# One block in each of eight groups gathered by the sync engine, row by row, in a graph attention and expert kernel

## The chip, the cores and the metric
The kernel runs on one core of a Trainium2 chip. The metric is its time on the device in microseconds, as the median of several runs; beside it stands the profile of one execution, whose span is measured from its first to its last instruction. The engines are named as in the profile: PE (matmuls), PEld (weight loads of PE), DVE, ACT, POOL (GpSimd) and SP (the sync engine). SPq rows are instructions that SP's queue issues.

## What is computed
A graph attention layer over 3125 nodes and 50000 edges, sorted by target `dst`, and behind it a layer of eight experts. Every edge needs the row of its source node: 256 features and 8 attention scores.

```python
h = (x @ W).reshape(N, H, C)                       # x: layer-normed nodes, N=3125, H=8, C=256
e = leaky_relu(a_src[src] + a_dst[dst], 0.2)
e = exp(e - segment_max(e, dst)[dst])
alpha = e / (segment_sum(e, dst)[dst] + 1e-16)
out = segment_sum(h[src] * alpha[:, :, None], dst).mean(axis=1) + bias
x = x + out
x = x + moe(layernorm(x))                          # top 2 of 8 experts, gelu between two 256x256 layers
```

## The kernel before, in words
The normed node features and the source scores are stored in a table in HBM, `node_table`, 264 floats a row (`TILES*P` rows). The edges are cut in 392 blocks of `BLK` = 128, and the blocks in nine groups by `GROUP_PLAN`: seven of 48 blocks, one of 32, one of 24. The ring in SBUF, `rows`, has `ROOM` = 96 slots of a block, one edge to a partition.

POOL gathers a block with one indirect DMA (`gather`, L730 to L736): 128 rows at the indices `idx[:, b]`. It goes through the groups in order. From group 2 it waits at every fourth block until PE is done with the blocks that stood in these slots (`block_done`). In group 0 it gathers 32 blocks, then sends 25 scatters of scores (L788) and a gather of start rows, then the other 16 blocks.

DVE does for each group g, in program order: `flags(g)` (from the scan line `dst_scan[g % 2]`, target numbers of the group; the first instruction, L1619, counts `scan_read`), `scores(g)` (L1641, waits until all blocks of the group have landed, semaphore `got`), the softmax steps, and `spreads(g)`, which makes PE's weights four blocks at a time. At g = 6 there is an exception: `flags(6)`, `flags(7)` and `flags(8)` stand one after the other, all ahead of `scores(6)`. PE multiplies a block in four matmuls (L973) and starts a group when its first weights are there. ACT drains sums and stores them in `agg_table`. When all groups are through, PE projects the sums (L1097) and the experts follow.

SP issues its transfers in program order. In the stretch with the groups these are: `node_scores_stored` (L568) and the score table (L571), the zeroed starts read back (L575, waits for the 25 scatters), a bias and four small weights (L577 to L581), and then `load_scan(g)` for g = 2 to 8 (L551, L554, L557), each of which waits until `flags(g - 2)` has read the buffer:

```python
n, ch = kb_of(g) * BLK, chunks_of(g)
if g >= 2:
    sp.wait_ge(scan_read, g - 1)
...
for g in range(2, GROUPS):
    load_scan(g)
```

The order on DVE at the end of the groups:

```python
for g in range(GROUPS):
    if g < GROUPS - 2:
        flags(g)
    if g == GROUPS - 3:
        flags(GROUPS - 2)
        flags(GROUPS - 1)
    ...
    scores(g)
```

Of the kernel before, what the change touches and what calls it, by code (L numbers as in the profile page):

```python
# [11 lines left out]
PE, POOL = mybir.EngineType.PE, mybir.EngineType.Pool  # L12
# [33 lines left out]
UNROLL = 5  # L46

# [17 lines left out]
def gat_moe_kernel(nc, x, src, dst, W, att_src, att_dst, gnn_bias, router_w, w1, b1, w2, b2, out):  # L65
# [68 lines left out]
    with ExitStack() as ctx:  # L134
# [125 lines left out]

        start_rows = sb("start_rows", [TURN_ROWS, H])
# [167 lines left out]
        got = [sem(f"got{j}") for j in range(4)]  # L429
        e_ready, eT_done, pieces_ready, pieces_done, fac_ready, fac_done = (  # L430
# [79 lines left out]
        def got_by(g):  # L510
            return 16 * sum(blocks_of(i) for i in range(g + 1) if got_of(i) == got_of(g))
# [4 lines left out]
        def _(sp):  # L516
# [46 lines left out]
            for i in range(TILES // UNROLL):  # L563
                sp.wait_ge(xn_ready, (i + 1) * UNROLL)
                sp.dma_start(node_table[:, 0:D].rearrange("(t p) d -> p t d", p=P)[:, i * UNROLL:(i + 1) * UNROLL, :],
                             xn[:, i * UNROLL:(i + 1) * UNROLL, :]).then_inc(xn_stored, 16)
            sp.wait_ge(score_ready, 1)
            sp.dma_start(node_table[:, D:].rearrange("(t p) h -> p t h", p=P), score_all[:, :, 0:H])\  # L568
                .then_inc(node_scores_stored, 16)
            sp.wait_ge(score_ready, 2)  # L570
            sp.dma_start(score_table.rearrange("(t p) h -> p t h", p=P), score_all[:, :, H:2 * H])\  # L571
                .then_inc(target_scores_stored, 16)

# [4 lines left out]
            for k in range(2):  # L578
                sp.dma_start(router_sb[:, k, :], router_w[:, k * P:(k + 1) * P].rearrange("e p -> p e"),
                             allow_slow_non_contiguous=True).then_inc(in_small, 16)  # L580
                sp.dma_start(b1_sb[:, :, k], b1[:, k * P:(k + 1) * P].rearrange("e p -> p e"),  # L581
                             allow_slow_non_contiguous=True).then_inc(in_small, 16)
            for g in range(2, GROUPS):
                load_scan(g)

# [82 lines left out]
        def _(pool):  # L668
# [61 lines left out]
            def gather(g, first, last):  # L730
                for s in range(first, last):
                    if g >= 2 and s % QUAD == 0:
                        pool.wait_ge(block_done, first_of[g] - ROOM + s + QUAD + 1)
                    b = first_of[g] + s
                    pool.indirect_dma_start(rows[:, slot_of(b), :], None, node_table,  # L735
                                            bass.IndirectOffsetOnAxis(idx[:, b:b + 1], 0)).then_inc(got[got_of(g)], 16)  # L736
# [608 lines left out]
        def _(dve):  # L1345
# [288 lines left out]
            def scores(g):  # L1634
# [3 lines left out]
                dve.wait_ge(got[got_of(g)], got_by(g))  # L1638

# [503 lines left out]
```

## Time and profile before
| | us |
|---|---|
| median of three runs | 1154.89 |
| lowest and highest | 1150.71, 1158.80 |
| span of the profiled execution | 1025.7 |
| busy: PE, DVE, ACT, POOL | 669.8, 680.2, 355.3, 673.2 |
| gathers of node rows (L735), 392 | 408.7 busy |
| largest items of the chain that ended last, by line | POOL L735 22%, PE L1097 12%, PE L973 5% |

The table's last rows are from the page of the profile. "Busy" doesn't count waits, nor the issuing of DMAs by SP and ACT. The groups are gathered from 57.7 us to 620.8 us of the span.

### The profile page before, as it was taken

How to read it: one execution, taken by the hardware profiler on the slowest of the kernel's cores; microseconds unless marked ns; L12 is line 12 of the kernel's file. 1: busy time of each engine (PE TensorE's matmuls, PEld its weight loads, DVE VectorE, ACT ScalarE, POOL GpSimd, SP SyncE). 2: the span in 40 equal slices, each digit the busy share in tenths (PEclk: the TensorE clock that was granted, in tenths of full speed). 3: DMA queues.
4: the chain of work that ended last, by engine and by line, in shares of the span. 5: the costliest groups of instructions: out<-in, count | busy, mean ns of one | idle time of the engine just before them, and what ended most of it. 6: DMA issues, size and time to landing. Idle time of an engine off the chain costs nothing.

```text
span 1025.7 us, 15575 instructions
## 1 busy us (share of the span) xinstructions
PE 669.8 (65%) x3740; PEld 602.6 (59%) x3741; DVE 680.2 (66%) x1860; ACT 355.3 (35%) x831; POOL 673.2 (66%) x705
## 2 busy tenths in 40 slices
PE   4982012427646275471754687599999998678996
PEld 3981001327546175461654677588888887567995
DVE  6888318727757276572875778657678968775663
ACT  3720003337645364231331110023323222335664
POOL 5787777777777777777777771235073375557786
PEclk9999999978878687676876898899999999889998
DMA  9634153567867677555664456198986862366873
GB/s 347 217 80 96 24 117 103 163 223 255 260 204 241 206 249 220 168 180 156 187 182 134 142 165 254 40 337 310 346 321 225 298 230 83 80 133 99 134 130 58
DMA packets 96985, 189.62 MB, mean 185 GB/s; under 512 B 24743, under 2 KB 54802, under 8 KB 95804
## 3 DMA queue, kind: packets, MB, share of 16 engines
q0 software_dynamic: 31680, 70.52, 28.3%
q1 hardware_dynamic: 50256, 72.93, 21.0%
q10 hardware_dynamic: 14960, 45.16, 11.4%
q8 instruction: 35, 0.57, 0.2%
q14 instruction: 54, 0.44, 0.1%
HBM read 124.74 MB, written 64.74 MB: 185 GB/s over the span
## 4 chain that ended last, share of the span: by engine, by line
PE 29%; POOL 26%; DVE 19%; issue 13%; DMA 8%; ACT 1%; POOLq 1%; DVEq 1%; ACTq 0%; SPq 0%; PEldq 0%; PEld 0%
POOL ring L735 22%; PE banks L1097 12%; PE banks L973 5%; PE banks L1172 3%; PE banks L1156 3%; DMA ring<-node_table,idx 3%; POOL starts_table L788 2%; DMA out<-ring 2%; PE banks L927 2%; DVE arena L1373 2%; DMA ring<-agg_table 1%; PE banks L914 1%; DMA arena<-in_src 1%; POOL slot_table L835 1%; PE banks L1144 1%
## 5 line engine op out<-in xcount | busy, mean ns | idle before, releaser
L735 POOL DMA_INDIRECT ring<-node_table,idx x392 | 408.7, 1043 | 121.4 <-issue 115.0
L973 PE MATMUL banks<-arena,ring 128*128 128x160 f32 x1568 | 256.9, 328 | 39.3 <-ACT banks L1264 18.7
L973 PEld LDWEIGHTS banks<-arena,ring 128*128 128x128 f32 x1568 | 245.2, 212 | 51.8 <-issue 51.4
L1258 ACT COPY arena<-banks 128x400 f32<-128x400 f32 x200 | 88.4, 493 | 322.6 <-PE banks L973 204.9
L1097 PE MATMUL banks<-ring 128*128 128x256 f32 x544 | 120.5, 381 | 0.0
L849 POOL DMA_INDIRECT out<-ring x56 | 89.8, 1603 | 33.9 <-DMA out<-ring 18.0
L1097 PEld LDWEIGHTS banks<-ring 128*128 128x128 f32 x544 | 102.7, 190 | 13.2
L1758 DVE TENSOR_TENSOR arena<-hot,arena 128x640 f32<-128x640 f32 x84 | 64.6, 823 | 34.8 <-PE banks L973 34.5
L980 PE MATMUL banks<-ident,edge_e 128*128 128x128 f32 x25 | 7.2, 417 | 119.7 <-DVEq L1649 119.6
L980 PEld LDWEIGHTS banks<-ident,edge_e 128*128 128x128 f32 x25 | 3.9, 201 | 121.9 <-DVEq L1649 121.9
L1156 PEld LDWEIGHTS banks<-ring 128*128 128x128 f32 x448 | 60.6, 200 | 20.0 <-DVE ring L2022 16.8
L1156 PE MATMUL banks<-ring 128*128 128x128 f32 x448 | 63.3, 287 | 13.2 <-DVE ring L2022 13.0
L835 POOL DMA_INDIRECT slot_table<-arena,slots x50 | 57.2, 1143 | 14.5 <-issue 13.7
L1172 PE MATMUL banks<-arena,ring 128*128 x224 | 62.4, 403 | 1.5 <-issue 1.4
L1641 DVE TENSOR_TENSOR edge_z<-ring,arena 128x384 f32<-128x384 f32 (+2 forms) x9 | 4.3, 478 | 82.4 <-DMA ring<-node_table,idx 82.4
L1097 PE MATMUL banks<-ring,arena 128*128 128x256 f32 x256 | 57.0, 381 | 0.0
L830 POOL COPY arena<-tags 128x3 f32<-128x3 f32 x25 | 3.6, 194 | 80.6 <-DVEq L1910 80.6
L1262 ACT COPY banks<-zeros 128x400 f32<-128x400 f32 x100 | 50.4, 504 | 11.6 <-ACT arena L1258 10.2
L1097 PEld LDWEIGHTS banks<-ring,arena 128*128 128x128 f32 x256 | 48.4, 190 | 6.3
L2046 DVE SCALAR_TENSOR_TENSOR ring<-banks,job_w,ring 128x256 f32<-128x256 f32 x56 | 27.1, 484 | 35.8 <-PE banks L1172 29.7
L1264 ACT COPY banks<-zeros 128x400 f32<-128x400 f32 x100 | 49.7, 497 | 0.0
L1172 PEld LDWEIGHTS banks<-arena,ring 128*128 128x128 f32 x224 | 40.2, 200 | 7.1 <-issue 3.4
(411 smaller groups left out, 1183.1 us busy)
## 6 DMA issues: line engine op xcount, KB each, us to landing
agg_table<-arena ACTq DMA_DIRECT2D x100, 400.0 KB
ring<-agg_table SPq DMA_DIRECT2D x25, 1600.0 KB, 8.5
ring<-slot_table SPq DMA_DIRECT2D x56, 130.0 KB, 2.6
ring<-node_table,idx POOLq DMA_INDIRECT x392
ring<-in_x SPq DMA_DIRECT2D x8, 640.0 KB, 13.2
arena<-in_L_ffn_w SPq DMA_DIRECT2D x16, 256.0 KB, 8.7
node_table<-ring SPq DMA_DIRECT2D x5, 640.0 KB, 5.4
ring<-in_L_gnn_W ACTq DMA_DIRECT2D x1, 2048.0 KB, 9.0
```

What stands on the lines that cost most here:

```text
L735: pool.indirect_dma_start(rows[:, slot_of(b), :], None, node_table, bass.IndirectOffsetOnAxis(idx[:, b:b + 1], 0)).then_inc(got[got_of(g)] ...
L835: pool.indirect_dma_start(slot_table, bass.IndirectOffsetOnAxis(slots[:, k, t:t + 1], 0), tn[t % TN_RING], None).then_inc(sent[t % TN_RING ...
L849: pool.indirect_dma_start(out, bass.IndirectOffsetOnAxis(xs[j % XS_RING][:, D:D + 1].bitcast(I32), 0), ybuf[j % Y_RING], None, bounds_chec ...
L973: m = pe.matmul(columns[:, k, bass.ds(at * (UNIT * H), SPREAD * H)], lhs[:, k * P:(k + 1) * P], weights, start=False, stop=True, skip_grou ...
L1097: m = pe.matmul(bank[proj_bank(t)][:, 0:D], aggt[t % AGG_RING][:, k * H + h, :], W_sb[:, k, h * C:(h + 1) * C], start=(k == 0 and h == 0), ...
L1156: m = pe.matmul(h_bank[j % 2][:, f * P:(f + 1) * P], w1_now[j % 2][:, k, f * P:(f + 1) * P], xsT[j % 2][:, k, :], start=(k == 0), stop=(k ...
L1172: m = pe.matmul(y_bank[j % 2][:, 0:D], h_sb[j % 2][:, f, :], w2_sb[:, bass.ds(e, 1), f, :].rearrange("p e n -> p (e n)"), start=(f == 0), ...
L1258: act.copy(stage[j][:, k * SLOTS * H:(k + 1) * SLOTS * H], views[k]).then_inc(drained, 1)
L1262: act.copy(views[0], zeros[:, 0:1].to_broadcast([P, SLOTS * H]))
L1264: act.copy(views[1], zeros[:, 0:1].to_broadcast([P, SLOTS * H])).then_inc(acc_free, 1)
L1758: dve.tensor_tensor(spread[:, s:s + QUAD, :].rearrange("p s (d h) -> p s d h", h=H), hot[:, q * QUAD:(q + 1) * QUAD, :].unsqueeze(3).to_br ...
L2046: dve.scalar_tensor_tensor(ybuf[j % Y_RING], y_bank[j % 2][:, 0:D], job_w[j % 3][:, 1:2], b2_now[j % 3], ALU.mult, ALU.add).then_inc(y_rea ...
```

## The change
SP gathers block 3 (`SP_AT`, the last of the first four) of groups 0 to 7. For each it loads the 128 source numbers of the block into `sp_src` (two buffers, `load_sources`), reads eight of them at a time into registers, and issues one DMA of one row (264 floats) for each edge, to the slot and partition where POOL's gather would have put it. POOL leaves these eight blocks out; DVE waits for both before `scores(g)`.

```diff
+ROWS_OF_SP = range(0, 8)
+SP_AT = QUAD - 1
+SP_WORDS = 8
+SP_FIRST = 48
...
         def got_by(g):
-            return 16 * sum(blocks_of(i) for i in range(g + 1) if got_of(i) == got_of(g))
+            return 16 * sum(blocks_of(i) - (i in ROWS_OF_SP) for i in range(g + 1) if got_of(i) == got_of(g))
...
+            def gather_rows(g, first, last):
+                b = first_of[g] + SP_AT
+                if first == 0:
+                    sp.wait_ge(in_sp_src, 16 * (g + 1))
+                    if g + 1 in ROWS_OF_SP:
+                        load_sources(g + 1)
+                    if g >= 2:
+                        sp.wait_ge(block_done, b - ROOM + 2)
+                for j0 in range(first, last, SP_WORDS):
+                    cols = slice(g % 2 * BLK + j0, g % 2 * BLK + j0 + SP_WORDS)
+                    _, nodes = nc.values_load_multi_w_load_instructions(sp_src[0:1, cols], engines=[SP], min_val=0, max_val=N - 1,
+                                                                       skip_runtime_bounds_check_because="every entry of src is a node")
+                    for n, node in enumerate(nodes):
+                        j = BLK - 1 - (j0 + n)
+                        sp.dma_start(rows[j:j + 1, slot_of(b), :], node_table[bass.ds(node, 1), :]).then_inc(got_sp[g % 2], 16)
+
+            def load_sources(g):
+                at = EP - (first_of[g] + SP_AT + 1) * BLK
+                sp.dma_start(sp_src[0:1, g % 2 * BLK:(g % 2 + 1) * BLK], src[at:at + BLK].rearrange("(i n) -> i n", i=1))\
+                    .then_inc(in_sp_src, 16)
+
+            load_sources(0)
             sp.wait_ge(score_ready, 1)
             sp.dma_start(node_table[:, D:].rearrange("(t p) h -> p t h", p=P), score_all[:, :, 0:H])\
                 .then_inc(node_scores_stored, 16)
+            sp.wait_ge(node_scores_stored, 16)
+            sp.wait_ge(xn_stored, 16 * (TILES // UNROLL))
+            sp.wait_ge(va_summed, 2)
+            gather_rows(0, 0, SP_FIRST)
             sp.wait_ge(score_ready, 2)
             sp.dma_start(score_table.rearrange("(t p) h -> p t h", p=P), score_all[:, :, H:2 * H])\
                 .then_inc(target_scores_stored, 16)
+            gather_rows(0, SP_FIRST, BLK)
...
+            sp.wait_ge(steps_ready, 1)
+            gather_rows(1, 0, BLK)
             for g in range(2, GROUPS):
                 load_scan(g)
+                if g in ROWS_OF_SP:
+                    gather_rows(g, 0, BLK)
...
                     b = first_of[g] + s
+                    if g in ROWS_OF_SP and s == SP_AT:
+                        continue
...
                 dve.wait_ge(got[got_of(g)], got_by(g))
+                if g in ROWS_OF_SP:
+                    dve.wait_ge(got_sp[g % 2], 16 * BLK * (g // 2 + 1))
```

SP's queue before, from the four small loads to the end of the groups; the scan lines of groups 2 to 8 stand together (`x5` and the three rows behind it):

```order
L579 DMA router_sb<-in_L_ffn_router_w 128x8x1
L581 DMA b_sb<-in_L_ffn_b 128x8x1
L551 DMA dst_scan<-dst_table 128x1x386 [waits scan_read] x5
L551 DMA dst_scan<-dst_table 128x1x258 [waits scan_read]
L554 DMA dst_scan<-dst_table 88x1x258 [waits scan_read]
L557 DMA dst_scan<-dst_table 8x257
L608 DMA ring<-in_L_gnn_W 128x2x2048 [waits block_done]
```

SP's queue now, at the start of group 1's rows (line numbers are those of the changed file; ISA is the register instruction that forms an address):

```order
L614 DMA router_sb<-in_L_ffn_router_w 128x8x1
L616 DMA b_sb<-in_L_ffn_b 128x8x1
L593 DMA sp_src<-in_src 1x128 [waits in_sp_src,steps_ready]
L585 TENSOR_LOAD sp_src
L589 ISA
L589 DMA ring<-node_table 1x264
L589 ISA
L589 DMA ring<-node_table 1x264
```

A block is 16 such TENSOR_LOADs, each followed by eight pairs of ISA and DMA. At the end of group 7's rows there stands now:

```order
L589 ISA
L589 DMA ring<-node_table 1x264
L562 DMA dst_scan<-dst_table 88x1x258 [waits scan_read]
L565 DMA dst_scan<-dst_table 8x257
L647 DMA ring<-in_L_gnn_W 128x2x2048 [waits block_done]
```

The scan line of group 8 (L554 and L557 before, L562 and L565 now) stands behind the 128 rows of group 7, whose first waits for PE's first four blocks of group 5; each of the scan lines of groups 3 to 7 stands behind the rows of the group ahead of it.

## Rows read from the trace of the kernel before
**Rows 1.** The page: the span, and the chain that ended last, by line.
```profile
span 1025.7 us, 15575 instructions
...
POOL ring L735 22%; PE banks L1097 12%; PE banks L973 5%; PE banks L1172 3%; PE banks L1156 3%; DMA ring<-node_table,idx 3%; POOL starts_table L788 2%; DMA out<-ring 2%; PE banks L927 2%; DVE arena L1373 2%; DMA ring<-agg_table 1%; PE banks L914 1%; DMA arena<-in_src 1%; POOL slot_table L835 1%; PE banks L1144 1%
```
**Rows 2.** Grouped by line, 164 to 547 us: count, busy us, mean ns, idle before.
```profile
L735 POOL DMA_INDIRECT ring<-node_table,idx x288 | 293.8, 1020 | 89.7 <-issue 85.2 <-PE banks L973 4.6
```
**Rows 3.** Waits, DVE's and SP's queue: us in total, times, longest.
```profile
DVE edge_z L1641 <- DMA ring<-node_table,idx: 82.4, 9, 16.5
...
SPq L551 <- DVE arena L1619: 310.4, 6, 66.1
```
**Rows 4.** Timeline of DVE: start us, duration us, what, idle before.
```profile
528.23 0.56 DVE L1619 TENSOR_TENSOR arena<-dst_scan 128x385 f32<-128x385 int32 x1
...
536.39 0.43 DVE L1619 TENSOR_TENSOR zero_rows<-dst_scan 128x257 f32<-128x257 int32 x1
...
548.76 0.56 DVE L1641 TENSOR_TENSOR edge_z<-ring,arena 128x384 f32<-128x384 f32 x1 [8.98 <-DMA ring<-node_table,idx]
...
592.85 0.43 DVE L1641 TENSOR_TENSOR edge_z<-ring,arena 128x256 f32<-128x256 f32 x1 [0.18 <-DMA ring<-node_table,idx]
...
626.39 0.36 DVE L1641 TENSOR_TENSOR edge_z<-ring,arena 128x192 f32<-128x192 f32 x1 [2.04 <-DMA ring<-node_table,idx]
```
**Rows 5.** Timeline of SP's queue: score table, starts, last small load, last scan line.
```profile
86.39 0.36 SPq L571 DMA_DIRECT2D score_table<-score_all  x1
...
139.11 0.34 SPq L575 DMA_DIRECT2D arena<-starts_table  x1
...
150.19 1.18 SPq L581 DMA_DIRECT2D b_sb<-in_L_ffn_b  x1
...
528.81 0.85 SPq L554 DMA_DIRECT2D dst_scan<-dst_table  x1
529.70 0.47 SPq L557 DMA_DIRECT2D dst_scan<-dst_table  x1
```
**Rows 6.** Timeline (first row), then single lines: count, ns min/median/max, first and last start.
```profile
2.08 0.55 SPq L524 DMA_DIRECT2D arena<-in_dst  x2
...
L524 SPq DMA_DIRECT2D arena<-in_dst x2: 228/255/282, 2.1 to 2.4; - x2
...
L654 SPq FUSED_REGOPS  x8: 37/37/42, 899.7 to 907.8; - x8
L654 SPq MOVE slot_table<-zero_rows x8: 29/29/29, 899.8 to 907.8; - x8
L654 SPq DMA_DIRECT2D slot_table<-zero_rows x8: 332/332/370, 899.8 to 907.9; - x8
...
L653 SPq TENSOR_LOAD <-fill_row x8: 263/270/507, 899.1 to 906.9; - x8
...
L841 POOLq TENSOR_LOAD <-job_wait x55: 315/326/604, 884.4 to 1016.1; - x55
...
L740 POOLq TENSOR_LOAD <-far x9: 289/296/889, 211.8 to 652.1; - x9
```
**Rows 7.** Timeline of PE: group 5 begins; the projection begins.
```profile
516.46 5.83 PE L973 MATMUL banks<-arena,ring 128*128 128x160 f32 x26 [2.52 <-DVE arena L1758]
...
668.37 3.83 PE L1097 MATMUL banks<-ring 128*128 128x256 f32 x17
```
**Rows 8.** DMA issues: KB each, median us from issue to landing.
```profile
dst_scan<-dst_table SPq DMA_DIRECT2D x1, 129.0 KB, 3.9
```
**Rows 9.** The page, DMA queues: packets, MB, share of 16 engines.
```profile
q0 software_dynamic: 31680, 70.52, 28.3%
q1 hardware_dynamic: 50256, 72.93, 21.0%
q10 hardware_dynamic: 14960, 45.16, 11.4%
```

More of the change, by code:

```diff
@@ L11 @@
 AX_X = mybir.AxisListType.X
-PE, POOL = mybir.EngineType.PE, mybir.EngineType.Pool
+PE, POOL, SP = mybir.EngineType.PE, mybir.EngineType.Pool, mybir.EngineType.SP
 P = 128
@@ L259, in gat_moe_kernel @@
         zero_rows = sb("zero_rows", [P, SLOT])
+        sp_src = sb("sp_src", [1, 2 * BLK], I32)
         start_rows = sb("start_rows", [TURN_ROWS, H])
@@ L429, in gat_moe_kernel @@
         got = [sem(f"got{j}") for j in range(4)]
+        in_sp_src = sem("in_sp_src")
+        got_sp = [sem(f"got_sp{j}") for j in range(2)]
         e_ready, eT_done, pieces_ready, pieces_done, fac_ready, fac_done = (
```

## The prediction
> **What bounds the kernel now.** I read the page first: its span, and the chain that ended last by line [rows 1]. POOL's gather at L735 is the largest item of the chain, 22%, three times any DMA item and ahead of every matmul line. Then the grouped instructions between 164 and 547 us, which is where groups 1 to 6 are gathered [rows 2]: 288 gathers, 293.8 us busy and 89.7 us idle, of which 85.2 is "issue", time in which POOL waited for nothing. So POOL gathers without a break: (293.8 + 89.7) / 288 = 1.33 us for one block of 128 edges, 64 us for a group. No other engine is near full in that stretch. The waits say the same from the other side [rows 3]: DVE waits nine times, once for each group, 82.4 us in all, for gathered rows to land. In the stages before and after (scores, projection, experts) the change alters nothing but what arrives late.
>
> Two more things must be read, because the change puts much work on the SP queue. First, what SP does in that stretch: it waits, 310 us in six waits at L551, for DVE to have read the last `dst_scan` buffer at L1619 [rows 3]. It looks like an idle queue. Second, what hangs on SP's few transfers there. DVE's timeline [rows 4] shows it for group 6: at 528.23 DVE reads the scan line of group 6 (flags), at 536.39 already that of group 8, and only behind that comes `scores(6)` at 548.76, after 8.98 us of waiting for the gather, so flags(8) ended at 539.78. The program has flags(6), flags(7), flags(8) ahead of scores(6) on DVE. The scan line of group 8 was sent by SP at 528.81 and 529.70 [rows 5], as soon as flags(6) had freed the buffer. So the cover of that transfer is 9 us and no more.
>
> **The change, part by part.**
> *Removed:* eight gathers on POOL, at 1.33 us each: 10.6 us. This is the whole possible gain; since POOL has no break, each of them would come off the end if all else kept up. Block 3 of groups 0 to 5 is 8.0 us of it, of groups 0 to 6 9.3 us.
>
> *Added on SP:* eight blocks of 128 single-row DMAs. None is in the trace of before, so I build the pitch of one row from its nearest rows [rows 6]. A register-addressed DMA of SP (L654) takes FUSED_REGOPS 0.037, MOVE 0.029 and the DMA itself. The DMA is 0.332 there for 128 partitions; the four single-row DMAs of L524 take 0.228 to 0.282, median 0.255. Two of them in a row take 0.55, so the gap between instructions is 0.55 - 0.51 = 0.04, three per row. Pitch: 0.037 + 0.029 + 0.255 + 3 x 0.04 = 0.44 us. I take the single-row duration because shape is what differs here, and registers seem to cost nothing extra in the DMA. The bounds are 0.41 (the 0.228) and 0.52 (the 0.332). For each 8 rows there is a TENSOR_LOAD: 0.27 for one word; POOL's loads of four words take 0.326 against 0.296 for one, 0.01 a word, so 0.32 for eight, 0.36 with a gap. A block is R = 128 x 0.44 + 16 x 0.36 = 56.4 + 5.8 = 62.2 us. (Bounds: 58 and 73.) That is just under POOL's 64 us a group: SP goes from idle to saturated.
>
> *Where the rows run:* group 0's are cheap. The first 48 go from 57 to about 80, ahead of the score store whose data came at 86; the other 80 need 39 us more, to 126; SP would wait until 139.11 for L575 anyway [rows 5]. All that moves is 1.3 us earlier. The four small loads behind L575 keep SP until 151.37; less 1.3 is 150.1, where rows(1) begin. From here SP is one chain: each later group adds a scan line (0.5, as the one at 529.70 [rows 5]), one load of addresses (0.255) and gaps, 0.85 in all. Rows of group 7 end at 150.1 + 0.3 + 6 x 0.85 + 7 x 62.2 = 590.9. The other condition, that rows(7) wait for the first four blocks of group 5 on PE (516.46 [rows 7], less 8.0, plus 16 matmuls at 5.83 / 26 us, 3.6, makes 512.1), would give 512.1 + 62.2 = 574.3, so the queue binds. Ends of rows(2) to rows(6), 276, 339, 402, 465 and 528, lie ahead of POOL's own gathers (before 290 to 547, less up to 9.3), so `scores` of groups 1 to 6 don't wait for rows.
>
> *Moved:* the scan line of group 8. It is now issued behind rows(7), at 590.9 in place of 528.81. Who is queued behind it: SP sends its two DMAs (1.36 us), they land 3.9 us after issue [rows 8], DVE's flags(8) take 539.78 - 536.39 = 3.4, and then only may scores(6) start: 590.9 + 8.7 = 599.6, against 539.5 if nothing were late. DVE, and behind it PE's group 6, stand still for that time, with POOL's gathers of groups 7 and 8 (its first 16) done meanwhile.
>
> *After that:* scores(6) to scores(7) is 592.85 - 548.76 = 44.1, set by DVE itself (0.18 of waiting). Scores(7) to scores(8) is 33.5, of which 2.04 was waiting for the gather [rows 4]; that is now early (the last eight gathers of group 8 need PE's second quad of group 6, 15 us before they are due), so 31.5. Scores(8) begins at 599.6 + 75.6 = 675.2, against 626.39: 48.8 us later. Behind it there is PE's group 8 and then, from 668.37, the projection [rows 7], both moved by the same amount.
>
> *Sum:* the POOL saving is used up in the wait; the end moves by +48.8. The profiled execution spans 1025.7 us; the runs have a median of 1154.9, so 129.2 us lie around the span, and nothing in the change touches them. 1154.9 + 48.8 = 1203.7, span 1074.5.
>
> What the skill says of such rows: the Trainium skill, DMA: Bandwidth & Descriptors, "Why a DMA increments its semaphore by 16 and not by 1", says that a single-row DMA may run on one DMA engine alone, always the lowest-numbered. By that rule all 1024 rows share one ring; no row here names an engine, and its price is the third rival's below, worked out from rows.
>
> **Range of the main case.** With the 0.228 DMA and 0.31 a load R is 58, the queue ends at 561.5 and PE's condition binds: 512.1 + 58 = 570.1, scores(6) 578.8, +28: 1183. With the 0.332 DMA R is 73, rows(7) end at 666, scores(6) at 675, +124: 1279. Every 0.01 us of pitch is 9 us at the end.
>
> **Rivals.**
> 1. *Each row costs SP a full-size DMA (0.52 us a row).* For it: 128-partition DMAs in this kernel agree at 0.33 to 0.37 and the four short ones are from the first microseconds, before any traffic. Against: the short ones had 2048 and 1344 bytes in one partition, which is the same shape. 1279, or about 1230 to 1290.
> 2. *No change, or faster: SP keeps up.* If rows(7) took less than 30 us, scan line 8 would be issued by 542.1 and the end would not move (542.1 + 8.7 + 75.6 = 626.4, scores(8) as before); below 18.7 us the full 10.6 us come, 1144.3. That needs 0.10 us a row, less than half of the shortest DMA instruction in the trace. This decides the sign: above 0.2 us a row the kernel is slower. A way in which it could still be: SP's instruction durations overlap. L654's eight DMAs start 1.16 us apart with 0.33 of DMA and 0.27 of load in each, more than the durations seen, so they don't.
> 3. *The rows are bound where they are moved, not issued.* Packet times from the page [rows 9]: q1 0.21 x 16 x 1025.7 / 50256 = 0.069 us, q0 0.147, q10 0.125. If all rows were on one ring with two packets each (data, semaphore), and each packet waited for one of q0 and one of q10, a row would take 2 x 0.341 = 0.68, R = 87, rows(7) end at 764, +222: 1377. Unloaded it is 2 x 0.069 = 0.14, far below the pitch of issue. The queues' shares (28.3, 21.0 and 11.4% over the span) say that a packet of each isn't waiting twice per row. The round that this assumes, one packet of each queue in turn, is the rule of the Trainium skill, DMA: Bandwidth & Descriptors, "Queues, rings and completion order"; no row shows it.
> 4. *Only the order bites.* R is smaller than built, some 45 to 57 (addresses found sooner, loads overlapping), and PE's condition sets rows(7): +15 to +27, 1170 to 1182.
>
> **How the numbers follow.** Main case (1183 to 1230) 0.60; rival 1 (1230 to 1290) 0.17; rival 4 0.09; rival 3 0.06; rival 2 0.08, of which within 1% 0.05 and over 1% faster 0.03 (the removed gathers alone are 0.9%, so this needs gathers that also run faster). A measurement of this kernel tells about 1% from no change, 11.5 us. Slower: 0.60 + 0.17 + 0.09 + 0.06 = 0.92. The time predicted is the main case's, 1204. Range 1180 to 1280: the bounds of the pitch; it leaves out rivals 2 and 3 and most of 4, about 0.2. The main case alone: 1183 to 1230.
>
> **What the profile after will show.** SP's single-row DMAs at 0.25 each and 0.44 apart; rows(1) from 150 to 213; rows(7) ending near 591; the scan line of group 8 issued right behind; DVE idle before its third L1619-type read of that group for some 50 us, released by `dst_scan<-dst_table`; nine POOL groups 1.3 us shorter each; PE idle from about 560 to 631 and its clock perhaps lower behind it; POOL gathers of unchanged length. I am wrong if SP's pitch is not 0.41 to 0.52, if DVE does not stand before flags(8), or if `scores` of an early group waits for `got_sp` (then the ring, rival 3, or rival 1 holds).

## The result, and the profile of the changed kernel

| kernel | median, us | range, us | against before |
|---|---|---|---|
| before, beside it | 1153.2 | 1150.7 to 1158.8 | |
| changed | 1424.3 | 1421.0 to 1435.6 | 1.2365, 95% interval 1.2313 to 1.2418 |

The changed kernel is slower by 271 us, where the prediction had 49 (1204, range 1180 to 1280). The sign was right; the size was wrong by a factor of five and the time lies outside the range.

The page of the changed kernel: its span, packets by queue, and the chain that ended last by engine and by line. It answers [rows 1, 9].
```profile
span 1422.4 us, 18781 instructions
...
q1 hardware_dynamic: 52320, 74.02, 15.6%
...
SPq 38%; issue 25%; PE 21%; DVE 9%; another core or an unknown queue 3%; DMA 2%; ACT 1%; DVEq 0%; POOLq 0%; ACTq 0%; PEldq 0%; PEld 0%; POOL 0%
SPq L589 31%; PE banks L1138 10%; SPq L585 6%; PE banks L1014 3%; PE banks L1197 3%; PE banks L1213 3%; PE banks L1185 1%; DVE ring L1436 1%; DMA ring<-agg_table 1%; DVE ring L1488 1%; PE banks L1158 1%; DVE stats L1472 1%; DMA arena<-in_src 1%; DVE arena L1414 1%
```
POOL's gather, 22% of the chain before, is gone from it. SP's queue has its place: L589 (the rows) and L585 (the register loads) are 37%. The waits (us in total, times, longest) say who waits for it, where [rows 3] had gathers:
```profile
DVE edge_z L1684 <- DMA ring<-node_table: 121.8, 5, 32.6
...
DVE zero_rows L1660 <- DMA dst_scan<-dst_table: 64.6, 1, 64.6
...
DVE arena L1660 <- DMA dst_scan<-dst_table: 33.8, 1, 33.8
```
The 64.6 us are the wait that the prediction named, in its place. The first row is the one by which it said that it would be wrong: scores of early groups wait for SP's rows.

What SP's instructions cost, by line: count, ns min/median/max. First in a stretch in which POOL issues 57 DMAs, then in one in which it issues none.
```profile
L589 SPq MOVE ring<-node_table x17: 4/700/1426, 150.4 to 219.7; - x17
L589 SPq DMA_DIRECT2D ring<-node_table x16: 690/700/1396, 152.5 to 216.9; - x16
L589 SPq FUSED_REGOPS  x16: 15/700/709, 154.6 to 218.3; - x16
...
L589 SPq MOVE ring<-node_table x77: 29/29/29, 856.0 to 895.9; - x77
L589 SPq DMA_DIRECT2D ring<-node_table x77: 224/225/261, 856.1 to 896.0; - x77
L589 SPq FUSED_REGOPS  x76: 37/37/37, 856.4 to 895.8; - x76
```
In 856 to 896 the prices are near those of the prediction: 0.225 us for the DMA (forecast 0.255), 0.029 and 0.037 as forecast. In 150 to 220 an instruction takes 0.70 us by the median, with as much between two, a register move of 29 ns too: 16 rows in 70 us. From the first of its row DMAs to the end of the last, a block took 192 us (group 0), 79 (group 1), 94 to 101 (groups 2 to 6) and 66 (group 7, while POOL waited for PE). The slowing is not there from POOL's first DMA at 64.07: from 65 to 70 us POOL issues 4 DMAs and SP starts 30 instructions; from 110 to 115 POOL again issues 4, and SP starts 5.

Nothing in the rows of before looks like that. The runs below show what it goes with: **the time depends on the chip.** The kernel before took 1142 to 1159 us on chips 2 and 13 and 1027 to 1034 us in 16 runs on chip 4. The chip of the first result isn't on record; its times of before are like those of chips 2 and 13. The trace that the prediction was read from, with its span of 1025.7 us [rows 1], looks like one of chip 4. Each comparison below is with runs of before on the same chip, unless it says otherwise.

### The profile page after: what moved, and what is told of

It reads as the page before. It is cut to its first block, busy times and chain, and to the rows that moved or that the text cites. A ratio compares the mean times of both kernels' runs of the same rounds, so it can differ in the third digit from the quotient of the medians.

```text
span 1422.4 us, 18781 instructions
## 1 busy us (share of the span) xinstructions
PE 703.8 (49%) x3740; PEld 633.4 (45%) x3741; DVE 678.6 (48%) x1860; ACT 354.9 (25%) x831; POOL 651.7 (46%) x697
## 4 chain that ended last, share of the span: by engine, by line
SPq 38%; issue 25%; PE 21%; DVE 9%; another core or an unknown queue 3%; DMA 2%; ACT 1%; DVEq 0%; POOLq 0%; ACTq 0%; PEldq 0%; PEld 0%; POOL 0%
SPq L589 31%; PE banks L1138 10%; SPq L585 6%; PE banks L1014 3%; PE banks L1197 3%; PE banks L1213 3%; PE banks L1185 1%; DVE ring L1436 1%; DMA ring<-agg_table 1%; DVE ring L1488 1%; PE banks L1158 1%; DVE stats L1472 1%; DMA arena<-in_src 1%; DVE arena L1414 1%
## 5 line engine op out<-in xcount | busy, mean ns | idle before, releaser
L776 POOL DMA_INDIRECT ring<-node_table,idx x384 | 390.5, 1017 | 500.7 <-PE banks L1014 354.9
L1014 PE MATMUL banks<-arena,ring 128*128 128x160 f32 x1568 | 290.4, 352 | 112.0 <-issue 57.4
L1014 PEld LDWEIGHTS banks<-arena,ring 128*128 128x128 f32 x1568 | 274.9, 232 | 126.8 <-issue 126.5
L1005 PE MATMUL banks<-ident,arena 98*128 98x98 f32 x32 | 7.3, 384 | 117.9 <-DVE arena L1643 117.9
L876 POOL DMA_INDIRECT slot_table<-arena,slots x50 | 54.1, 1081 | 14.5 <-issue 13.7
L1005 PEld LDWEIGHTS banks<-ident,arena 98*128 98x128 f32 x32 | 4.9, 217 | 120.5 <-DVE arena L1643 120.5
L1275 ACT COPY arena<-banks 128x392 f32<-128x392 f32 x8 | 6.9, 858 | 205.6 <-PE banks L1005 205.6
```

Of the source, the lines that this page charges most:

```text
L876: pool.indirect_dma_start(slot_table, bass.IndirectOffsetOnAxis(slots[:, k, t:t + 1], 0), tn[t % TN_RING], None).then_inc(sent[t % TN_RING ...
L1014: m = pe.matmul(columns[:, k, bass.ds(at * (UNIT * H), SPREAD * H)], lhs[:, k * P:(k + 1) * P], weights, start=False, stop=True, skip_grou ...
```

## The experiments

**Theory A:** SP's instruction stream is slowed while POOL issues indirect DMAs, whatever its instructions are. **Theory B:** the transfers of the rows are held back in their queue. With either goes the prediction's order term: group 8's scan line behind the rows of group 7. In what follows rows(g) are SP's 128 row DMAs for group g, and "the starts" are the start rows that SP reads back once POOL's 25 scatters are through.

### Order, addresses, DMAs: four kernels on chip 13

*Scan line of group 8 first.*
```diff
             for g in range(2, GROUPS):
-                load_scan(g)
+                if g < GROUPS - 1:
+                    load_scan(g)
+                if g == GROUPS - 2:
+                    load_scan(GROUPS - 1)
                 if g in ROWS_OF_SP:
                     gather_rows(g, 0, BLK)
```


> The scan line of group 8 is issued ahead of group 7's rows on SP instead of behind them; nothing else changes. Theory A (SP's instruction stream is slowed while GpSimd issues its own indirect loads) and theory B (the transfers of SP's rows are held back in their queue) both leave the rows' pace alone and expect the order's share of the loss back: scores of group 8 then no longer wait for rows(7), which end at 915.4, but for its own flags at 918, so only the aggregation tail moves; 20 to 50 us, thus 1375 to 1405 us. If the order were the whole of the loss (the prediction's own term) it would come to under 1200 us.

Measured: 1384.6 us beside 1151.0 (1.2009, 1.1950 to 1.2069). The order is worth some 40 us of the 271, no more (1424.3 less 1384.6; the chip of the first is not known).

*Fixed rows.*
```diff
-                    _, nodes = nc.values_load_multi_w_load_instructions(...)
-                    for n, node in enumerate(nodes):
+                    for n in range(SP_WORDS):
                         j = BLK - 1 - (j0 + n)
-                        sp.dma_start(rows[j:j + 1, slot_of(b), :], node_table[bass.ds(node, 1), :])...
+                        at = (b * BLK + j) % N
+                        sp.dma_start(rows[j:j + 1, slot_of(b), :], node_table[at:at + 1, :])...
```


> SP still issues 128 one-row loads per block of groups 0 to 7, but at fixed rows of the node table: no word is read into a register and no address is computed, so some 128 instructions a block stand where some 400 stood (these blocks then hold other nodes' rows). Theory A, a price for each SP instruction while GpSimd issues: a block falls from 98 us to about a third to a half of it (33 to 50 us), SP is ahead again in the loop of groups 2 to 7, and the kernel comes to 1180 to 1300 us. Theory B, a price for each transfer in the queue: a block stays near 98 us and the kernel near 1400 us (1380 to 1430).

Measured: 1195.7 us (1.0383, 1.0322 to 1.0444). The same 1024 transfers, but a third of the instructions: a block now takes 44 to 56 us in groups 2 to 7, and some 229 of the 271 us are gone. Theory B had 1400. The rows are also neighbours in the table here, so by this run alone their addresses could be the cause; the next one has no rows at all.

*No row DMAs at all.*
```diff
-                    for n, node in enumerate(nodes):
-                        j = BLK - 1 - (j0 + n)
-                        sp.dma_start(rows[j:j + 1, slot_of(b), :], ...).then_inc(got_sp[g % 2], 16)
+                    for n in range(3 * SP_WORDS):
+                        sp.sem_inc(got_sp[g % 2], 1)
```


> SP issues no row loads; 384 increments of a semaphore stand on SP in the place of each block's registers and loads, GpSimd loads every block as before the change, and nobody waits for SP's increments. Theory A: they too are stretched while GpSimd issues, SP reaches each scan line late, and the kernel is clearly above the one before: 1200 to 1400 us. Theory B: without transfers nothing is held back; an increment takes some 0.04 us, a block 15 us, and the kernel stays within 1% or so of the one before (1145 to 1170 us).

Measured: 1248.7 us (1.0859, 1.0812 to 1.0905). Increments that nobody waits for, with no transfer behind them, cost 98 us, because SP's scan lines and the load of the starts stand behind them. Theory B is out. The increments in two stretches of this kernel, with POOL gathering and with POOL idle, and in a third just after POOL's last gather for the time (issued at 224.16):
```profile
L588 SPq EVENT_SEMAPHORE  x50: 5/700/714, 149.9 to 220.0; - x50
...
L588 SPq EVENT_SEMAPHORE  x309: 17/17/17, 256.0 to 276.0; - x155
...
L588 SPq EVENT_SEMAPHORE  x8: 3/694/700, 225.6 to 235.3; - x8
```
So 1.4 us an increment against 0.065; and the slowing outlasts POOL's last issue by some 10 us. DVE, which waits for the starts, begins scores of group 0 at 269.1.

*Group 7 alone.* `ROWS_OF_SP = [7]`, with SP's buffers and counts to match.

> SP loads the one block of group 7 alone; the other seven are GpSimd's again. It prices the order at the end (scan line of group 8 behind rows of group 7) with a block at the pace it has there. Theory A: group 7's rows fall where GpSimd gathers, so the block takes 90 to 100 us from about 530 and ends at 620 to 630: scores of groups 7 and 8 come 70 to 85 us late, 1215 to 1240 us. Theory B, with no backlog from earlier groups in the queue: the block takes the undisturbed 66 us, ends at about 596, and the kernel comes to 1185 to 1210 us.

Measured: 1211.7 us (1.0522, 1.0475 to 1.0570), +61. The value lies between the two theories' (1215 to 1240 and 1185 to 1210): the 8 rows from 638.9 to 649.2 took 10 us, with up to 0.7 for an instruction; from 650 on 8 rows took 3.1 to 3.5 us, the full pace, although POOL issued until 660. So the slowing isn't there whenever POOL issues.

### The base again: four kernels on chip 4

*The kernel before again.*

> The kernel before, unchanged, profiled again: its page shows a span of 1025.7 us, while its timed runs stand at 1151 to 1159, and the other kernels' spans here are 2 to 3 us below their times. If the 129 us lie around the span, as the prediction took it, this run shows a span of about 1026 us again at a time near 1151. If that one execution was itself a quick one, the span is 1144 to 1154 us, scores of group 0 start near 225 us (as in the kernel with group 7 alone) instead of 165.3, and the comparisons of stages have to be made against this run.

Measured: 1030.7 us with a span of 1029.0. Neither case as I had put it: the time itself is short, with 1.7 us around the span.

*Increments on SP and ScalarE in the kernel before.*
```diff
             gather(0, 0, FIRST_GATHERS)
+            pool.sem_inc(pool_there, 1)
...
+            act.wait_ge(pool_there, 1)
+            for n in range(200):
+                act.sem_inc(idle_incs[0], 1)
...
+            sp.wait_ge(pool_there, 1)
+            for n in range(100):
+                sp.sem_inc(idle_incs[1], 1)
             sp.wait_ge(starts_sent, 16 * TILES)
```


> The kernel before with nothing of the change, but with bare semaphore increments that nobody waits for, released when GpSimd has issued its first 32 loads (about 110 us): 100 on SP ahead of the wait for the starts, 200 on ScalarE, which is idle there. It asks whether only SP is slowed or any engine. If the slowing is SP's own, SP takes 0.7 to 1.4 us for each while GpSimd issues (so the 100 end after 210 us and the loads of the starts come late by 50 to 80 us), ScalarE 0.04 to 0.06 us (200 in about 10 us). If every engine's short instructions are slowed, both go at 0.7 to 1.4 us. If increments alone are not slowed (it needed the row loads or the registers), both end within 15 us and the time is that of before within 1%.

Measured: 1034.1 us beside 1032.6; SP (L578) and ScalarE (L1240):
```profile
L578 SPq EVENT_SEMAPHORE  x100: 17/17/20, 89.7 to 96.1; - x100
...
L1240 ACTq EVENT_SEMAPHORE  x200: 17/17/17, 89.7 to 103.7; - x100
```
No slowing, with POOL issuing its first loads until 105. That is no evidence for theory B; it is another chip.

*Plain loads on POOL* (increments on SP as above).
```diff
-                    pool.indirect_dma_start(rows[:, slot_of(b), :], None, node_table,
-                                            bass.IndirectOffsetOnAxis(idx[:, b:b + 1], 0))...
+                    at = b * BLK % (N - BLK)
+                    pool.dma_start(rows[:, slot_of(b), :], node_table[at:at + BLK, :])...
```


> As the kernel without row loads (384 increments on SP for each block), but GpSimd's 392 loads of 128 rows are plain loads of fixed rows instead of indirect ones (so the blocks hold other nodes' rows); the same bytes go the same way. If it is GpSimd's work on indirect loads that holds SP back, SP takes 1.4 us for 24 increments throughout the loop, and the kernel loses its 96 us over before, or nearly (1130 to 1190 us, plus what GpSimd's own issue changes). If it is the traffic of the loads, SP's pace stays at 5 to 10 us for 24 increments and the time near 1250 us.

Measured: 944.0 us. On this chip there was no slowing to take away, so it doesn't tell the trigger. It points at what bounds the kernel before here: a plain load keeps POOL 0.56 us, an indirect one 1.02, and the time is 89 us less (the plain loads also read neighbouring rows, so the 89 aren't shown to be POOL's alone). The kernel computes something else, since its blocks hold other nodes' rows.

*Group 0 alone.* `ROWS_OF_SP = [0]`.

> SP loads the one block of group 0 alone; groups 1 to 7 are GpSimd's again. It prices the start. The prediction had it hidden (within 1% of before, 1145 to 1165 us). By theory A the rows end near 245 to 257 us, the starts are read 100 to 112 us later than in the kernel before, and with the 20 us or so for which other work would have waited anyway the kernel comes to 1225 to 1260 us.

Measured: 1031.9 us beside 1032.6, one run of each: hidden, as the prediction said. POOL was gathering group 0's first blocks meanwhile, and rows cost what they should.

### The changed kernel on chip 4

The rest is between **theory C** (on some chips all short instructions are stretched while POOL issues indirect DMAs, on others none) and **theory D** (it is this kernel's, anywhere).

> The changed kernel, unchanged, run again, because the kernel before stood at 1151 us beside the runs so far with 3 rounds and at 1032 us beside the four with one look (on another chip). If the conditions of the chip decide (theory C: there is a condition in which each engine's short instructions are stretched while GpSimd issues indirect loads, and one in which they are not), then on a chip where the kernel before takes about 1032 us the rows go at 4.1 us for 8 throughout, as in the kernel with group 0 alone, and the prediction's own sum holds: 1032 + 49 = 1081 us, 1060 to 1100. Where the kernel before takes about 1151 us, it comes to 1424 us again. Theory D, that the SP stream suffers in this kernel anywhere: over 1250 us beside a before of 1032 us.

Measured: 1130.2 us beside 1029.2 (1.0968, 1.0928 to 1.1008). Neither 1081 nor over 1250: the stretch is gone, and a loss of 101 us is left, twice the predicted 49. Its rows and register loads on SP (count, ns min/median/max, first and last start):
```profile
L589 SPq FUSED_REGOPS  x1024: 37/37/51, 57.4 to 644.1; - x171
L589 SPq MOVE ring<-node_table x1024: 29/29/39, 57.4 to 644.2; - x171
L589 SPq DMA_DIRECT2D ring<-node_table x1024: 221/225/924, 57.5 to 644.2; - x171
...
L585 SPq TENSOR_LOAD <-sp_src x128: 689/786/1962, 56.5 to 640.4; - x128
```
The timeline of SP's queue, for [rows 5]: the load of the starts, and scan lines.
```profile
138.28 0.32 SPq L610 DMA_DIRECT2D arena<-starts_table  x1
220.11 0.59 SPq L559 DMA_DIRECT2D dst_scan<-dst_table  x1
293.02 0.55 SPq L559 DMA_DIRECT2D dst_scan<-dst_table  x1
...
576.82 0.54 SPq L559 DMA_DIRECT2D dst_scan<-dst_table  x1
644.49 0.88 SPq L562 DMA_DIRECT2D dst_scan<-dst_table  x1
```
The timeline of DVE, for [rows 4]: scores(5), flags(7), flags(8), scores(6), scores(8).
```profile
509.09 0.43 DVE L1684 TENSOR_TENSOR edge_z<-ring,arena 128x256 f32<-128x256 f32 x1 [22.89 <-DMA ring<-node_table]
...
580.03 0.43 DVE L1660 TENSOR_TENSOR arena<-dst_scan 128x257 f32<-128x257 int32 x1 [22.37 <-DMA dst_scan<-dst_table]
647.49 0.43 DVE L1660 TENSOR_TENSOR zero_rows<-dst_scan 128x257 f32<-128x257 int32 x1 [63.91 <-DMA dst_scan<-dst_table]
650.91 0.56 DVE L1684 TENSOR_TENSOR edge_z<-ring,arena 128x384 f32<-128x384 f32 x1
...
727.27 0.36 DVE L1684 TENSOR_TENSOR edge_z<-ring,arena 128x192 f32<-128x192 f32 x1
```
SP's scan lines are 71.3 us apart ((576.82 - 220.11) / 5), POOL's groups 1 to 4 are 61 to 63 us long. SP is the bound from group 2 on, and `scores` of groups 2 to 5 start 1.2 to 1.7 us behind SP's last row of their group.

*Group 8's scan line first,* on chip 4:

> The kernel with group 8's scan line ahead of group 7's rows, again. Where the kernel before takes 1032 us, theory C: groups 2 to 7 take 62 to 66 us on SP beside 61 to 64 us on GpSimd, so nothing but a few us a group is late and the tail's order is mended: 1032 to 1060 us, 20 to 45 us under the changed kernel. Theory D: 35 to 45 us under the changed kernel, both over 1200 us.

Measured: 1082.2 us (1.0498, 1.0450 to 1.0546). The order is worth 48.0 us here. 53 are left.

*Increments instead of row DMAs,* on chip 4:

> The kernel with 384 increments on SP per block and no row loads, again. Where the kernel before takes 1032 us, theory C: an increment takes some 0.06 us as in the kernel with bare increments, a block about 24 us, nobody waits: 1030 to 1040 us. Theory D: 1120 to 1140 us (96 us over before, as on the first chip).

Measured: 1031.8 us in one run beside 1029.2, where chip 13 had +98. The same instructions, in the stretch in which chip 13 did 50:
```profile
L588 SPq EVENT_SEMAPHORE  x692: 17/17/17, 151.2 to 220.0; - x173
```
Theory D is out; theory C's "none" on this chip stands.

*Group 7 alone,* on chip 4:

> The kernel with group 7's block alone on SP, again. Where the kernel before takes 1032 us, theory C: its rows start when the slot is free, near 528 us by the trace of before, and end 66 us later at 595; the scan line of group 8 is issued behind them and scores of group 7 wait for them: 1065 to 1085 us. It is the prediction's main term by itself; if it costs under 20 us the main term was wrong there too.

Measured: 1074.6 us, +45. The end of its rows (57 of them in the first row) and group 8's scan line:
```profile
560.06 29.07 SPq L591 DMA_DIRECT2D ring<-node_table  x57
589.18 0.88 SPq L562 DMA_DIRECT2D dst_scan<-dst_table  x1
```
This is the prediction's main term alone, and it is there: DVE waits 54.7 us before flags(8). That the line goes out at 589.2, where the prediction had 590.9, is luck. Here no earlier rows fill the queue; SP waits for PE's first blocks of group 5. For that condition the prediction had a start at 512.1 and a block of 62.2 us, hence 574.3; measured were 522 and 67.

### What chip 2 adds

The same increments on SP and ScalarE in the kernel before:

> The kernel before with 100 increments on SP and 200 on ScalarE, again. Where the kernel before takes 1029 us: as the first time, 0.06 us each and 1030 to 1036 us. Where it takes 1151 us: if SP alone is slowed, 0.7 to 1.4 us each there and 0.05 us on ScalarE; if every engine is, both are slow; 1190 to 1250 us in either case, as the starts are read behind SP's.

Measured: 1175.2 us, beside 1143 to 1159; less than I expected. Scores of group 0 begin at 251.4, only 26 us later than in the kernel before on this chip. Increments of SP and of ScalarE between 110 and 215 us:
```profile
L578 SPq EVENT_SEMAPHORE  x77: 690/700/1395, 109.7 to 214.7; - x77
...
L1240 ACTq EVENT_SEMAPHORE  x77: 14/700/711, 109.7 to 214.7; - x77
```
Both queues advance at the same 1.38 us an instruction. It is not SP's own: theory A in its first form falls. Seen closer, it is one beat for all. SP's and ScalarE's increments between 119.9 and 126.6 us, and DVE's short instructions there:
```profile
L578 SPq EVENT_SEMAPHORE  x5: 709/709/709, 120.2 to 125.8; - x5
...
L1240 ACTq EVENT_SEMAPHORE  x5: 700/700/700, 120.2 to 125.8; - x5
...
120.96 0.25 DVE L1570 TENSOR_TENSOR need_f<-need_f,arena 1x100 f32<-1x100 f32 x1 [1.14 <-DVE arena L1569]
122.36 0.26 DVE L1569 TENSOR_SCALAR arena<-need_f,bound_f 1x100 f32<-1x100 f32 x1 [1.15 <-DVE need_f L1570]
123.76 0.25 DVE L1570 TENSOR_TENSOR need_f<-need_f,arena 1x100 f32<-1x100 f32 x1 [1.14 <-DVE arena L1569]
```
All three engines start an instruction every 1.40 us there, at fixed distances from each other: of SP's 83 increments between 105 and 220 us, 77 end within 0.02 us of one of ScalarE's. POOL's DMAs follow each other every 1.28 us in the same stretch, so the beat isn't POOL's issue. And it isn't there at once: ScalarE's first 14 increments, from 96.75, go at 0.07 us each. SP suffers most only because the change gives it so many short instructions.

*The kernel before there:*

> The kernel before, unchanged. Where it takes 1151 us its trace tells what it loses itself: by theory C VectorE's many short instructions at the start, so that scores of group 0 begin near 225 us instead of 164, and the rest of the 120 us in groups 0 to 6, where other engines than GpSimd become the bound. Where it takes 1029 us it repeats the run of before.

Measured: 1141.9 us, span 1140.2. DVE's scores of groups 0, 6 and 8:
```profile
225.67 0.56 DVE L1641 TENSOR_TENSOR edge_z<-ring,arena 128x384 f32<-128x384 f32 x1
...
640.15 0.56 DVE L1641 TENSOR_TENSOR edge_z<-ring,arena 128x384 f32<-128x384 f32 x1
...
734.20 0.35 DVE L1641 TENSOR_TENSOR edge_z<-ring,arena 128x192 f32<-128x192 f32 x1
```
Beside chip 4's trace of the same kernel (163.92, 549.42, 628.20): 62 us at the start, 29 in groups 0 to 6, 15 behind them, together 106 of 111. At the start 7 us are there before POOL's first gather (63.94 against 57.27). The other 56 are a wait for PE: after the starts PE transposes the filled scores of eight heads (L964, four matmuls a head), ScalarE (ACT) copies each head once PE has signalled it, and flags(0) on DVE wait for all eight (57.1 us). The fourth and fifth copy here, then on chip 4:
```profile
176.26 0.81 ACT L1234 COPY arena<-banks 128x392 f32<-128x392 f32 x1 [9.68 <-remote]
187.49 0.81 ACT L1234 COPY arena<-banks 128x392 f32<-128x392 f32 x1 [10.41 <-remote]
...
153.65 0.84 ACT L1234 COPY arena<-banks 128x392 f32<-128x392 f32 x1 [0.27 <-PE banks L964]
154.76 0.85 ACT L1234 COPY arena<-banks 128x392 f32<-128x392 f32 x1 [0.28 <-PE banks L964]
```
The trace has the matmuls of one head 1.12 us behind those of the one before on both chips, but on chip 2 the semaphore events of PE that the copies wait for come 11.2 us apart. A head is four weight loads and four matmuls, and eight times 1.40 is 11.2: the beat holds for PE too. I had expected VectorE's short instructions to be what is late; its chain ends at 125.2 here and at 111.3 on chip 4, both ahead of the starts. In the groups POOL now waits for PE (57.8 us between 160 and 640), so GpSimd is no longer alone the bound.

*Groups 0, 2, 4, 6* (`ROWS_OF_SP = [0, 2, 4, 6]`), same chip:

> SP loads the fourth block of groups 0, 2, 4 and 6 alone. Where the kernel before takes 1029 us: if what is left of the loss is that SP's 70 us for a block exceed GpSimd's 63 us for a group, each block now has some 127 us, its rows end before GpSimd's, and nothing waits; GpSimd leaves out 4 of 392 loads of 1.33 us: 1022 to 1030 us, at best 5 us faster than before. If the rows cost in another way (transfers, the queue, the wait), half of the 53 us: near 1055 us. Where the kernel before takes 1151 us: rows at 98 us still fit into two groups but group 0's do not, 1200 to 1260 us.

Measured: 1266.7 us (1.0992, 1.0939 to 1.1045). Scores of group 0 begin at 281.6 instead of 225.7: half of the loss is the start. The question for which I made this kernel, whether anything waits on chip 4 when SP has two groups' time for a block, stays open: there is no run of it there.

*Four register loads a block,* group 8's scan line first:
```diff
-SP_WORDS = 8
-SP_FIRST = 48
+SP_WORDS = 32
+SP_FIRST = 32
```


> Group 8's scan line first, and one register load for 32 words instead of 8 (4 a block instead of 16; group 0's rows in parts of 32 and 96). If a load's 0.78 us hardly grows with the words, a block takes 4 x 0.8 to 1.6 + 128 x 0.41 = 56 to 59 us, with the 3 to 5 us of slower instructions that the blocks showed 59 to 64; with 2 us between blocks SP is level with GpSimd (63 us a group) and the kernel takes 1020 to 1040 us where the one before takes 1029. If a load's time goes by its words (3.1 us for 32), nothing changes: 1082 us as with 8 words.

Measured on chip 2: 1376.9 us beside 1151.5 (1.1956, 1.1903 to 1.2008), against 1384.6 with 8 words on chip 13. Stretched rows drown it. On chip 4:

> Group 8's scan line first and 4 register loads a block, again: its trace on the first try showed a load of 32 words at its own time. Where the kernel before takes 1029 us: 1020 to 1045 us if the length of SP's block (56 to 64 us instead of 68 to 72) was the whole of the 53 us that were left; 1070 or more if the rows cost in another way. Where the kernel before takes 1151 us: 1377 us again.

Measured: 1045.0 us beside 1032.0 (1.0125, 1.0103 to 1.0146), still slower. A load of 32 words takes 2.33 us by the median (min 2.05), against 0.79 for 8. A block with its loads takes 63 to 66 us in groups 1 to 7 instead of 68 to 73, the loss falls from 53 to 13 us, and the cause of the 53 is mostly shown by that: the length of SP's block. From block to block it is still 66 us ((548.9 - 218.5) / 5, the starts of rows(2) and rows(7)), 4 above POOL's 62.

*Plain loads on POOL,* on chip 4 again:

> The kernel with 384 increments on SP a block and plain loads of 128 fixed rows on GpSimd in place of its indirect ones, again (the blocks hold other nodes' rows). Where the kernel before takes 1151 us: if GpSimd's indirect loads are what slows the others, increments go at 0.06 us beside the plain loads and the kernel comes under 1000 us but for the scatters at the start; if any load that GpSimd issues does it, the increments stay at 0.3 us and more in the loop and the kernel is over 1150 us. Where it takes 1029 us it repeats 944 us.

Measured: 946.0 us, as the first time. There is no run with plain loads on chip 2 or 13. That POOL's *indirect* DMAs are the trigger is therefore not shown; it rests on the coincidence in time of the traces alone, and that is a loose one, with an onset behind POOL's and an end 10 us after it. All runs here, timed ones too, carry a recorded span; whether the stretch occurs in an unrecorded run is open as well. No version that gathers the right rows was clearly faster than the kernel before on either kind of chip.

## Why the prediction was right or wrong, point by point

Start of `scores` in the traces, us (0, 5, 6, 8 are groups):

| | 0 | 5 | 6 | 8 | time |
|---|---|---|---|---|---|
| before, chip 4 | 163.9 | 484.5 | 549.4 | 628.2 | 1030.7 |
| changed, chip 4 | 163.8 | 509.1 | 650.9 | 727.3 | 1130 (median) |
| before, chip 2 | 225.7 | 568.4 | 640.2 | 734.2 | 1141.9 |
| changed, first result | 280.9 | 745.3 | 921.9 | 1015.1 | 1425.2 |

**The step that failed** is the price of SP's instructions, R = 62.2 us a block. With its loads a block took 80 us in group 1, 94 to 102 in groups 2 to 6 and 193 in group 0 of the result, and 67 to 72 in groups 1 to 7 on chip 4. With R fell "just under POOL's 64 us", and with that the step that `scores` of groups 1 to 6 don't wait for rows. What made the chips differ stays open.

1. **"129.2 us lie around the span, and nothing in the change touches them": wrong.** Around the span lie 1.6 to 2.8 us. The 129 were the difference between two kinds of execution, like those of chip 4 and of chips 2 and 13: I took durations from one and added them to a time of the other. By itself this changes no term of the +48.8, but it hid that R was read where short instructions aren't slowed. For chip 4 the forecast would have read 1080; for the chip of the result no row of the trace was valid for short instructions.
2. **Pitch of a row, 0.44 us: near on chip 4** (0.41: 8 rows in 3.1 to 3.3 mostly), at the lower bound given. In the result it was 0.58 to 0.66 in groups 2 to 6 (the loads aside), and 4.4 in 150 to 220 (16 rows in 70 us). By the table, with chip 2 as base, the change costs 55 us at the start, 122 over groups 0 to 5, 105 from 5 to 6 (chip 4: 0, 25 and 77) and nothing behind. That is 283 us, since the base of the table is the fastest run of before on such a chip.
3. **A register load of 8 words, 0.32 us, from POOL's 1 and 4 words at 0.01 a word: wrong.** It took 0.79 by the median, 0.69 to 1.96, 12.5 to 17.0 us for the 16 of a block instead of 5.8. R came to 67.0 to 72.0 instead of 62.2, although the rows were cheaper than forecast. The Trainium skill, DMA: Bandwidth & Descriptors, "Latency and other measured facts", gives a register load a floor of some 600 ns. The 8-word loads are above it, one-word loads (0.263 [rows 6]) are not, so the measured rows by size decide. With its gaps a load and its eight rows take 4.1 us at the least, 1.0 of it the load. The load is why "ends of rows(2) to rows(6) lie ahead of POOL's own gathers" failed: 62.2 was under POOL's 64, 70 is over it, and so groups 2 to 5 waited too (25 us by `scores(5)`), and rows(7) ended at 644.4 instead of 590.9: 53.5 later. 49 + 53 makes 102, and chip 4 lost 101. The bound of R that I had given, 73 us and +124, would have held it.
4. **The moved scan line: right.** DVE waits 63.9 us before flags(8); `scores(6)` starts 6.5 us after rows(7) end (forecast 8.7); from there to `scores(8)` 76.4 (75.6). Reordering gives back 48.0 us on chip 4 and some 40 where short instructions are slowed.
5. **Group 0's rows hidden: right on chip 4** (group 0 alone: -0.7 us; the starts are read at 138.28, before 139.11). Wrong on the others: rows(0) last until 258.2 on chip 2, 257.5 on chip 13 and 256.9 in the first result, where the starts are read at 256.96, 112 us later than in the kernel before on chip 2 (144.98). `scores(0)` is 55 us late and not 112, since PE's eight heads then fall where POOL is idle, and ScalarE's copies of them are 1.1 us apart.
6. **Removed gathers, 1.33 us each: right and worthless** (POOL's groups 1 to 3 are 1.3 to 2.3 us shorter), since POOL is not the bound any more (107 us waiting for PE on chip 4, 355 in the result, before 6).
7. **Rivals.** SP keeps up (2) needed 0.10 us a row; it is 0.41. The ring (3) is out as the bound: there are two packets a row as assumed (q1 has 2064 more packets than before; among them 1024 of 1056 bytes, one for each row, so a row's data ran on one DMA engine), but without any row DMA 98 us were lost on chip 13, the same 1024 transfers at fixed addresses cost 45 there, and on chip 4 `scores` start within 1.7 us of SP's last row. Its 1377 is the nearest number to the result, by a mechanism that is not there. Rival 1 (0.33 a DMA) isn't either: the median is 0.225. Rival 4 named the order alone: it is 40 to 48 us, but never alone.
8. **Two slips of reading.** POOL's L735, 22% of the chain, is seven times the largest DMA item (3%) and not three times; and eight groups of POOL's are shorter by a gather, not nine. Neither changes the sum.

## What to carry to other kernels

Compare the profiled span with the timed runs first. Here 1.6 to 2.8 us lay between a run's time and its own span; a gap of 129 us was no overhead to be carried along but a sign that trace and times came from different conditions, and then the forecast has to be made for both. A queue that goes from idle to nearly as long as the bound's period is the fragile part of a change. Price each kind of instruction on it by its own size (a register load grows with its words), and treat a result of "just under" as over. And in an in-order queue nothing that a later stage waits for belongs behind a long stream: here one moved line of code gave back 40 to 48 us.

## What the runs showed of the hardware

- The same kernel takes 1030 us on chip 4 and 1142 to 1159 us on chips 2 and 13. On the latter there are stretches beside POOL's indirect DMAs in which SP and ScalarE advance by one instruction in 1.40 us, whatever the instruction (an increment of 17 ns, a move of 29 ns, a DMA of 225 ns), and VectorE's short instructions and the signals of PE's matmuls keep the same beat; POOL's own gathers keep their 1.0 us. The slowing isn't there from the first: in the first result SP still runs at nearly full pace between 65 and 70 us, with POOL gathering since 64, and is slowed to the full at 110; and it goes on for some 10 us after POOL's last gather.
- What makes a chip so isn't known here. One candidate is the recording itself: the Trainium skill, NOTIFIC — the notification-queue block, "7.1 Overflow: three behaviours, one of which stalls the engine", says that the block that writes an engine's records holds its producers back rather than lose one inside, and that this can throttle an engine. One beat for four engines and all kinds of instruction, 0.70 us at each end of one, a late onset and a backlog after POOL's last issue would fit. That is argued; no run here shows it, and all runs were recorded.
- SP issues a one-row DMA of a register's address in 0.41 us in all. A TENSOR_LOAD on SP took 0.27 us for 1 word [rows 6], 0.79 for 8 and 2.33 for 32 (medians).
- A plain DMA of 128 neighbouring rows keeps POOL 0.56 us, an indirect one of 128 rows 1.02.
